# A chain of graph and dense layers on one core: the recurrent cell's columns ordered by gate, and the ODE without filler behind its loop branch

## What is computed

```python
f = lambda z: _mlp(z, *params)          # tanh(z W1 + b1), tanh(. W2 + b2), W3
k1 = f(y)
k2 = f(y + dt / 2 * k1)
k3 = f(y + dt / 2 * k2)
k4 = f(y + dt * k3)
return y + dt * (k1 + 2 * k2 + 2 * k3 + k4) / 6
```

```python
i, f, g, o = jnp.split(gates, 4, axis=-1)
c_new = jax.nn.sigmoid(f) * c + jax.nn.sigmoid(i) * jnp.tanh(g)
h_new = jax.nn.sigmoid(o) * jnp.tanh(c_new)
```

## Time and profile before

| | us |
|---|---|
| median of three runs | 7168.47 (7166.38 to 7169.55) |
| profiled execution | 7165.25 |
| its span, first to last instruction | 7163.6 |
| ODE loops | 629.9 to 2389.5 and 2389.5 to 3377.9 |
| recurrent cell's loop, some 624 steps | 3669 to 6731 |
| PE busy | 6236.3 (87% of the span) |
| DVE, ACT, POOL busy | 2602.1, 1699.6, 895.0 |
| mean granted TensorE clock | 0.953 of full speed |

### The profile page before, as it was taken

One profiled execution on the slowest core, in us unless ns is written; L12 is line 12 of the kernel. 1 busy time (PEld: TensorE's weight loads), 2 busy tenths in 40 slices (PEclk: granted clock), 3 DMA queues, 4 the chain that ended last, 5 costly groups with the idle time before them and its releaser, 6 DMA issues. The chain is left out here.

```text
span 7163.6 us, 497293 instructions
## 1 busy us (share of the span) xinstructions
PE 6236.3 (87%) x212267; PEld 4149.4 (58%) x212267; DVE 2602.1 (36%) x12046; ACT 1699.6 (24%) x8390; POOL 895.0 (12%) x2042
## 2 busy tenths in 40 slices
PE   7857999999999999998789999999999999999831
PEld 5524555555555555554467777777777777777510
DVE  5324445454545211111233332333233332222267
ACT  0121333333333333333001111111111111111111
POOL 0011111111111584000000000000000000000000
PEclk9977999999999999999799999999999999999965
DMA  1011111111111110000232221222122211111100
GB/s 47 1 44 36 33 34 32 33 33 34 32 33 33 40 42 22 0 0 0 69 92 41 40 44 13 40 44 40 18 39 41 40 29 7 7 7 7 20 13 7
DMA packets 814786, 212.82 MB, mean 30 GB/s; under 512 B 706441, under 2 KB 772653, under 8 KB 814724
## 3 DMA queue, kind: packets, MB, share of 16 engines
q1 hardware_dynamic: 765700, 152.75, 11.1%
q0 software_dynamic: 47872, 54.13, 2.8%
q10 hardware_dynamic: 1152, 5.15, 0.2%
HBM read 183.50 MB, written 28.16 MB: 30 GB/s over the span
## 5 line engine op out<-in xcount | busy, mean ns | idle before, releaser
L1755 PE MATMUL ps_rows<-whh,h_pair 128*4 128x320 f16 x34944 | 1303.1, 299 | 85.7 <-issue 2.2
L1074 PE MATMUL ode_busy<-ode_busy_x,ode_busy_w 128*32 128x384 f16 (+4 forms) x18816 | 1253.8, 326 | 25.8 <-issue 14.8
L1755 PEld LDWEIGHTS ps_rows<-whh,h_pair 128*4 128x4 f16 x34944 | 739.9, 84 | 504.6 <-DVE h_pair L1613 155.7
L1068 PEld LDWEIGHTS ode_psa<-ode_a,ode_w2t 128*32 128x32 f32 x19968 | 421.5, 109 | 708.8 <-ACT ode_a L1181 562.8
L1625 DVE COPY gate_rows<-ps_rows_last 128x192 f32<-128x192 f32 x624 | 223.2, 358 | 1510.6 <-PE ps_rows_last L1755 1510.6
L1191 DVE SCALAR_TENSOR_TENSOR ode_part<-ode_b 128x1 f32<-128x1 f32 x624 | 110.6, 177 | 1608.1 <-ACT ode_b L1183 1608.1
L1677 ACT COPY gate_rows<-ps_rows 128x320 f32<-128x320 f32 x624 | 265.8, 426 | 1674.5 <-PE ps_rows L1755 1674.5
L1183 ACT ACTIVATE ode_b<-ode_psa 128x1 f32<-128x1 f32 x2496 | 427.4, 171 | 880.5 <-PE ode_psa L1068 880.5
L1068 PE MATMUL ode_psa<-ode_a,ode_w2t 128*32 128x1 f32 x19968 | 607.2, 180 | 1.0 <-issue 0.8
L1085 PE MATMUL ode_pso<-whh 125*32 125x170 f32 (+3 forms) x9600 | 564.3, 310 | 28.3 <-issue 28.3
L1799 PE MATMUL ps_gates<-l_gsel,gate_rows 128*32 128x4 f32 x19968 | 407.1, 177 | 137.9 <-DVE gate_rows L1625 128.5
(11 more groups left out here) (499 smaller groups left out, 9706.8 us busy)
## 6 DMA issues: line engine op xcount, KB each, us to landing
late_w<-in_wih_t SPq DMA_DIRECT2D x386, 128.0 KB, 2.1
xg_buf<-xg_scratch SPq DMA_DIRECT2D x1248, 16.0 KB, 2.0
split_raw<-in_whh_t SPq DMA_DIRECT2D x64, 256.0 KB, 2.6
ig_w<-in_wih_t SPq DMA_DIRECT2D x8, 2048.0 KB, 11.4
xg_scratch<-late_out SPq DMA_DIRECT2D x24, 624.0 KB, 3.2
whh<-h_scratch SPq DMA_DIRECT2D x105, 62.5 KB, 2.4
xg_scratch<-ig_out ACTq DMA_DIRECT2D x8, 628.0 KB, 8.0
h_scratch<-mlp_h SPq DMA_DIRECT2D x40, 125.0 KB, 2.3
```

Source lines behind the costliest of these rows:

```text
L1068: m = nc.tensor.matmul(ps[32 * j:32 * j + 32, 0:1], w[:, 32 * j:32 * j + 32], col, start=start, stop=stop, skip_group_check=True)
L1074: nc.tensor.matmul(ps_busy[32 * j:32 * j + 32, 0:cols], busy_w[:, 32 * j:32 * j + 32], busy_x[:, 0:cols], start=True, stop=True, skip_grou ...
L1755: m = nc.tensor.matmul(out[32 * j:32 * j + 4, :], hpair[:, c, 2 - 2 * part:6 - 2 * part], whh[:, at + lo:at + hi], start=(part == 0 and c ...
```

## The change

In the ODE, `SHADOW` becomes `UNITS + NT` = 85, so 15 turns go from the first loop to the second. Slot n = 0 is left empty in both loops; in the first loop the job pieces of slots 0 to 8 go to slots 1 to 9, where slot 9 was filler.

In the recurrent cell the weight columns of a product are ordered by gate: 256 columns for input and g gates, 128 for the forget gate, 128 for the output gate. One round of the first 256 columns is done ahead for each set instead of two of 320; two sets share a bank. Behind the choice come 7 rounds of 256, 8 rounds of 128 (`ps_rows_forget`), 8 rounds of 128 (`ps_rows_out`). VectorE copies the two blocks of 128 one after the other. The input's part is added by two matmuls with the whole identity as weights, 12 columns into `ps_gates` and 4 into `ps_out_gate`. The output gate has a PSUM tile, a semaphore and a tanh of its own, and `wsel_out_gate` is formed straight from that tanh, behind the cell state. Host layouts and scale factors follow.

```diff
-SHADOW = 100
+SHADOW = UNITS + NT
 def job_slot(n, cols):
-    if n < 6:
-        sum_piece(0, n // 3, n % 3)
-    elif n < 9:
-        weight_piece(1, n - 6)
+    if n == 0:
+        return
+    elif n < 7:
+        sum_piece(0, (n - 1) // 3, (n - 1) % 3)
+    elif n < 10:
+        weight_piece(1, n - 7)
-    steps_tensor(pe, i, lambda n, cols: busy(cols), lambda r, s: None)
+    steps_tensor(pe, i, lambda n, cols: busy(cols) if n else None, lambda r, s: None)
...
-    AHEAD = 2
-    FIRST = 5 * 64
+    AHEAD = 1
+    FIRST = 2 * 128
...
# VectorE, cell
-nc.vector.scalar_tensor_tensor(parts[:], act[:, 0:8], 1.0, act[:, 12:20], ALU.add, ALU.mult).then_inc(S["fi"], 1)
-nc.vector.tensor_scalar(ok[:], act[:, 8:12], 1.0, 1024.0, ALU.add, ALU.mult).then_inc(S["o"], 1)
+nc.vector.scalar_tensor_tensor(parts[:], act[:, 0:2 * KC], 1.0, act[:, 2 * KC:4 * KC], ALU.add, ALU.mult).then_inc(S["fi"], 1)
 v.wait_ge(S["fi"], k + 1)
 nc.vector.scalar_tensor_tensor(ccur, parts[:, KC:2 * KC], 0.5, parts[:, 0:KC], ALU.mult, ALU.add).then_inc(S["c_ready"], 1)
+v.wait_ge(S["out_acted"], k + 1)
+nc.vector.tensor_scalar(ok[:], out_tanh[:], 1.0, 1024.0, ALU.add, ALU.mult).then_inc(S["o"], 1)
+nc.vector.scalar_tensor_tensor(wgated[:], out_tanh[:].unsqueeze(2).broadcast_to([128, KC, PAIRS]), 1.0, wsel[:, 0:KC, :], ALU.add, ALU.mult).then_inc(S["w_ready"], 1)
 v.wait_ge(S["o"], k + 1)
-nc.vector.tensor_tensor(wgated[:], wsel[:, 0:KC, :], ok[:].unsqueeze(2).broadcast_to([128, KC, PAIRS]), ALU.mult).then_inc(S["w_ready"], 1)
...
# VectorE, step
-v.wait_ge(S["rows_last"], k)
-nc.vector.tensor_copy(gsb[:, FIRST:D], psb[:, 0:D - FIRST]).then_inc(S["evac_v"], 1)
+v.wait_ge(S["rows_forget"], k)
+nc.vector.tensor_copy(gsb[:, 256:384], psf[:, 0:128]).then_inc(S["evac_f"], 1)
+v.wait_ge(S["rows_out"], k)
+nc.vector.tensor_copy(gsb[:, 384:512], pso[:, 0:128]).then_inc(S["evac_o"], 1)
# ScalarE
-nc.scalar.activation(act[:, 0:16], psc[:, 0:16], ACT.Tanh).then_inc(S["acted"], 1)
+nc.scalar.activation(act[:, 0:IFG], psc[:, 0:IFG], ACT.Tanh).then_inc(S["acted"], 1)
+a.wait_ge(S["out_gate"], k + 1)
+nc.scalar.activation(out_tanh[:], psq[:, 0:KC], ACT.Tanh).then_inc(S["out_acted"], 1)
# PE, recurrent(e)
 for part in range(2):
     for c in range(KC):
-        m = products(e, part, c, psb[:, 0:D - FIRST], FIRST, D)
-m.then_inc(S["rows_last"], 1)
-for j in range(4):
-    m = nc.tensor.matmul(psc[32 * j:32 * j + 32, 0:16], ident[:, 32 * j:32 * j + 32], xgb[:, q, :, e * 8:(e + 1) * 8], start=True, stop=False, skip_group_check=True)
-m.then_inc(S["xg_used"], 1)
+        m = products(e, part, c, psf[:, 0:128], 256, 384, (part, c) == (0, 0))
+m.then_inc(S["rows_forget"], 1)
+for part in range(2):
+    for c in range(KC):
+        m = products(e, part, c, pso[:, 0:128], 384, 512, (part, c) == (0, 0))
+m.then_inc(S["rows_out"], 1)
+nc.tensor.matmul(psc[:, 0:IFG], ident[:], xgb[:, q, e * 16:e * 16 + IFG], start=True, stop=False, skip_group_check=True)
+nc.tensor.matmul(psq[:, 0:KC], ident[:], xgb[:, q, e * 16 + IFG:(e + 1) * 16], start=True, stop=False, skip_group_check=True).then_inc(S["xg_used"], 1)
# PE, turns
 pe.wait_ge(S["evac_a"], k)
-turn(0)
-turn(1)
-turn(2, (0, 1))
-pe.wait_ge(S["evac_v"], k)
-turn(2, (2, 3))
-turn(3).then_inc(S["gates"], 1)
+turn(psc[:, 0:KC], 0, False)
+turn(psc[:, 2 * KC:3 * KC], 1, False)
+pe.wait_ge(S["evac_f"], k)
+turn(psc[:, KC:2 * KC], 2, True).then_inc(S["gates"], 1)
+pe.wait_ge(S["evac_o"], k)
+turn(psq[:, 0:KC], 3, True).then_inc(S["out_gate"], 1)
```

More of the change, by code:

```diff
@@ L1732, in _ @@
                 pe.wait_ge(S["kept"], 1)
-                nc.tensor.matmul(psc[:, 0:16], ident[:], xg0[:], start=True, stop=True).then_inc(S["gates"], 1)
+                nc.tensor.matmul(psc[:, 0:IFG], ident[:], xg0[:, 0:IFG], start=True, stop=True).then_inc(S["gates"], 1)
+                nc.tensor.matmul(psq[:, 0:KC], ident[:], xg0[:, IFG:16], start=True, stop=True).then_inc(S["out_gate"], 1)
                 def turn_of_two(i, token):
@@ L1749, in turn_of_two, with products @@
                         m.then_inc(S["logits"], 1)
-                        def products(e, part, c, out, lo, hi):
+                        def products(e, part, c, out, lo, hi, start):
                             for j in range(4):
@@ L1755, in products @@
                                 m = nc.tensor.matmul(out[32 * j:32 * j + 4, :], hpair[:, c, 2 - 2 * part:6 - 2 * part], whh[:, at + lo:at + hi],
-                                                     start=(part == 0 and c == 0), stop=(part == 1 and c == KC - 1), skip_group_check=True)
+                                                     start=start, stop=(part == 1 and c == KC - 1), skip_group_check=True)
                             return m
                         def first(e, part, c):
-                            return products(e, part, c, psg[:, e * BANK:e * BANK + FIRST], 0, FIRST)
+                            return products(e, part, c, psg[:, e * FIRST:(e + 1) * FIRST], 0, FIRST, part == 0 and c == 0 and e % 2 == 0)
                         pe.wait_ge(S["hp_ready"], k)
@@ L1794, in turn_of_two, with turn, late @@
                                 recurrent(0)
-                        def turn(c, quarters=range(4)):
-                            for j in quarters:
-                                m = nc.tensor.matmul(psc[32 * j:32 * j + 32, c:16:4], gsb[:, c * 128 + 32 * j:c * 128 + 32 * j + 32], gsel[:], start=False, stop=(c == KC - 1), skip_group_check=True)
-                            return m
-                        pe.wait_ge(S["evac_a"], k)
-                        turn(0)
-                        turn(1)
-                        turn(2, (0, 1))
-                        pe.wait_ge(S["evac_v"], k)
-                        turn(2, (2, 3))
-                        turn(3).then_inc(S["gates"], 1)
-                        for c in range(q * PER, (q + 1) * PER):
-                            m = nc.tensor.matmul(ps_late[:, 0:BLOCK], late_w[:, c * 128:(c + 1) * 128], xt[:, c, ds(token, BLOCK)], start=(c == 0), stop=(c == KC - 1))
-                        m.then_inc(S["late_used"], 1)
+                        def turn(out, block_no, last):
+                            for j in range(4):
+                                m = nc.tensor.matmul(out[32 * j:32 * j + 32, :], gsb[:, block_no * 128 + 32 * j:block_no * 128 + 32 * j + 32], gsel[:, int(block_no == 1), :],
+                                                     start=False, stop=last, skip_group_check=True)
+                            return m
+                        def late(n):
+                            c = q * PER + n
+                            m = nc.tensor.matmul(ps_late[:, 0:BLOCK], late_w[:, c * 128:(c + 1) * 128], xt[:, c, ds(token, BLOCK)], start=(c == 0), stop=(c == KC - 1))
+                            if n == PER - 1:
+                                m.then_inc(S["late_used"], 1)
+                        pe.wait_ge(S["evac_a"], k)
+                        turn(psc[:, 0:KC], 0, False)
[4 more added lines that the diff above has]
+                        turn(psq[:, 0:KC], 3, True).then_inc(S["out_gate"], 1)
+                        late(0)
+                        late(1)
                 assert LOOPS == (BLOCKS + 1) * TURNS
@@ L2218, in lay_out @@
     a["pairs"] = pairs.reshape(128, PAIRS)
-    gsel = np.zeros((128, 4), np.float32)
-    for j in range(4):
-        half = 1.0 if j == 2 else 0.5
-        gsel[32 * j:32 * j + 2, GATE_SLOT[j]] = half * 2.0 ** -17
-        gsel[32 * j + 2:32 * j + 4, GATE_SLOT[j]] = half * 2.0 ** -28
+    gsel = np.zeros((128, 2, KC), np.float32)
+    for j in range(KC):
+        for b, half in enumerate((0.5, 1.0)):
+            gsel[32 * j:32 * j + 2, b, j] = half * 2.0 ** -17
+            gsel[32 * j + 2:32 * j + 4, b, j] = half * 2.0 ** -28
     a["gsel"] = gsel
```

51 lines of the change are left out of this document (27 added, 24 removed).

## The result

The changed kernel takes 12981.33 us (median of four runs, 12974.72 to 12988.48) where the kernel before took 7167.43 beside it: the ratio is 1.8112, 95% interval 1.8081 to 1.8144. The forecast was 7161 us, with a range of 7070 to 7300.

The account below looks back on a forecast made before the run. Serial chains in the ODE loops and recurrent cell, not TensorE's busy time, were taken as the bound. 7165.25 - 38 (ODE) + 31 (cell) = 7158 us profiled, with the median 3 us higher: 7161, range 7070 to 7300.

Parts of the forecast that it names:

- PE's code no longer stays: Cell loop: about 1820 instructions, one block fetched again per turn, 510 us more, 7670 us; chance 0.08.
- 38 forecast: ODE loops: no filler behind the branch and 15 turns changing loops save 38 us, ends 32 and 52.
- The 0.09 allowed for the branch's register arithmetic: ODE loop heads: the wait's register arithmetic behind the branch keeps 0.09 us of each turn's excess.
- My 0.34 for the first loop: First ODE loop: the head step's excess, 0.87 us tanh to tanh against 0.53 in a steady step.
- The rival that the excess stays: ODE loop heads: the branch alone sets the excess, so -5 us instead of -38, 7194 us; chance 0.06.
- the falling clock: PE idles more, clock falls to 1.2 GHz; every third ODE turn would cost 85 us, 7245 us; chance 0.08.
- +0.05 us a step: Recurrent cell: gate arithmetic at s + 3.81 against 3.76 before, +31 us over 624 steps.
- idle behind the choice: Cell: chosen rounds start at s + 1.10, with PE idle about 0.66 us in every step.
- the rival of the short rounds: Cell: rounds of 128 columns take 0.0825 us like those of 192, 0.42 us more a step, 7425 us; chance 0.09.
- The input passes: Cell, ahead of the turns: four passes of 128 weight columns at 0.109, less 0.05, about 0.39 us; 0.06 before.
- The rival that the four whole passes hide: Cell: input gates' passes cost the 0.06 us of before, chain 0.33 shorter, 6955 us; chance 0.11.
- the likeliest case: Whole kernel: ODE gains and the cell gives it back, 7161 us, own range 7075 to 7215; chance 0.58.

Follow-up runs that it names:

- forget and output as one: Changed kernel with the forget and output gates' rounds merged into 8 rounds of 256 columns, four copies of the chosen cell's code kept: 7266.95 us, ratio 1.0143.
- three copies: Changed kernel with three copies of the chosen cell's code instead of four, cells 0 and 1 sharing one, part of the results left out: 7205.98 us.
- one of 1629 that touches 8 blocks: Kernel before with 232 never-run instructions in the cell's loop and 96 instructions put ahead of it: 13263.58 us.
- In quarters: Kernel with three copies, input gates added by eight products of 32 weight columns instead of two of 128: 7038.4 us.

## Why the prediction was wrong

**The step that failed** is the fetching of PE's code: the sum has no term for it, and the rival that stands for it got a chance of 0.08 and a price of one block per turn, 510 us. The rival "PE's code no longer stays" was named and counted (1820 instructions, "more than any loop here has kept"; there are 1844). What happened is this rival, with all its blocks: 9 packets per turn. From the runs its price can be read: with short code and four copies 7267 us (forget and output as one), as it is 12981; 5714 us over 312 turns are 18.3 us a turn, 2.0 a packet. An estimate from the windows says where they go. In the turn shown PE idles 28.90 - 15.94 = 13.0 us; with three copies it is some 0.9 in a turn, (3150 - 2879)/310. So some 12 us are pauses for code, and the other 6 or 7 are PE's own work at the 1.2 GHz level, 15.9 us busy instead of 9.3.

What made a loop of 1820 look near the limit and not over it were two numbers. The ODE's turn of 1504 loads and matmuls stayed; with its branches and registers it lies in 7 blocks, the last number that does on these runs. The other was the figure of the Trainium skill (Runtime: NRT & Kernel Launch, "Instruction fetch mechanics"), 2048 instructions. The measurement decides: a loop of 1844 doesn't stay, nor one of 1629 that touches 8 blocks. And I asked what one block would cost, where the runs show that a loop that overruns fetches all its blocks in each turn.

**The ODE**: the mechanism right, the size too low. 48 us measured, 38 forecast, ends 32 to 52. A turn gains 17.487 - 17.19 = 0.30 us in the first loop and 17.343 - 17.07 = 0.27 in the second, where I had 0.25 and 0.21. The 0.09 allowed for the branch's register arithmetic has no run behind it and isn't there: the head's step takes 0.53 like the others. My 0.34 for the first loop came from one step, 0.87 long; over the 100 turns the median is 0.81, so the gain is the whole excess. One term stood at nothing in the sum: 8 of the second loop's 55 turns from 2413 us on were longer than 18 us, which costs some 10 us in all, and in the changed kernel one of 70 is. In the profiles the last turn of the ODE ends 61 us sooner (3377.5 before, 3316.5 after); the stage behind it lasts 278 to 289 us from profile to profile, so how much of the 61 a run keeps is open within the interval of 39 to 62. The rival that the excess stays is out. So is the falling clock as it was meant: the second loop goes through 65 turns at 17.07 us, and the cell with three copies runs at 1.00. Its sign, a clock of 0.5 in the cell, did come, but with the fetches.

**The cell, without the fetches**: slower than before by more than the +0.05 us a step that I had. From the kernel with three copies (s = 4700.26) the terms are: idle behind the choice to s + 0.95 (with one branch less; with four copies 1.08, forecast 1.10): right. Rounds of 256 at 4701.97 - 4701.21 = 0.76: right. Forget rounds 0.45: right, 0.056 each, and the rival of the short rounds is out. From the turns to the gate arithmetic 0.66, forecast 0.67: right. **The input passes**: mis-sized. Out rounds and passes take 4703.51 - 4702.42 = 1.09 us, forecast 0.45 + 0.39. The first pass comes 4702.97 - 4702.42 = 0.55 behind the first output matmul, 0.10 behind the end of the rounds if these take 0.45 as the forget rounds do, and a pass takes 0.135 and not 0.11. So the term is 0.64 and not 0.39, 0.25 us a step or some 156 us over 624. In quarters the passes take 0.12, and the run gets 168 us faster: the test of that term. The rival that the four whole passes hide is out; they stand in the open.

The Trainium skill (TensorE: Matmul & The Clock Gate, "Back-to-back issue gap") gives about 81 ns for a load-matmul pair at 128 columns. For rounds of four matmuls on four row groups the trace does not agree: a whole round of 128 columns takes 56 ns.

The forecast's centre would have been too low with code that stays, too. With four copies an estimate is 7270 to 7290 us: 7267 with forget and output as one, and 7206 + 624 x 0.13 = 7287 from three copies and the one branch less. The range of 7070 to 7300 would have held it, but by its width: the likeliest case ended at 7215. (From the ends of the two stages it should have been 7071 to 7206; nothing hangs on that.)

## What to carry to other kernels

Count the instructions of a loop's body on TensorE before it grows, untaken copies and all, in blocks of 16 KB: here a loop that touched 7 stayed, and one that touched 8 did not. The instruction packets in the DMA part of the page show at once whether a loop stays. If it is near the limit, shorten it (fewer, wider matmuls; a copy less, where the work allows it) or move it by a few dozen instructions. When a rival is a cliff, price the whole fall, not its first step.

## What was not expected of the hardware

- Placement alone: 96 instructions ahead of a loop took 7209 to 13264 us, 160 gave 7212.
- In the ODE, with less work behind the branch, the clock falls less often and not more: the 65 turns between 2207 and 3299 us take 17.07 us, where 8 of the 55 turns of the second loop before took 18.2 to 19.0 (the earlier trace rows has one).
- Four passes with 128 weight columns stand in the open at the end of a stream of row-group rounds (0.54 us, and 0.10 us of wait in front), where the same sums in eight products of 32 columns take 0.12.
